# Two-layer cross-attention: the value bias summed under the attention by VectorE, one output product for two batches

## The chip, the cores and the metric

The kernel runs on 1 core of one Trainium2 chip. The metric is the device time of one execution in microseconds (us). The kernel before took 1253.28 us (median of 3 runs, 1253.11 to 1253.95).

## The reference

Two layers follow one another. The change is in the first. Its inputs are `x` and `ctx` (the `y` below), 32 batches of 128 channels by 1024 columns:

```
q, k = Wq y + bq, Wk y + bk;   v = Wv x + bv          # 8 heads of 16 channels
scores = q k^T / sqrt(128)                            # over the 1024 columns: 16x16 per head
attn = softmax(scores)
o = Wo (attn v) + bo + x
h = (o - mean(o)) * rsqrt(var(o) + 1e-5) * gn_w + gn_b   # mean and variance over a whole batch
```

The second layer is an attention with 32 heads over `h` and `ctx`, with low-rank additions to its weights; its output is added to `h`.

## The kernel before, in words

In the first layer the scores don't need q and k themselves. They come from the Gram matrix of a batch, y y^T (128x128), through the weights. The attention of a batch, `att`, is one 128x128 matrix with the heads on its diagonal. Then `n1` = att^T Wo^T and `mix` = Wv^T n1, plus the identity, so that the first layer's output before the norm is mix^T x plus one column, `xbias`:

xbias = Wo (att bv) + bo = n1^T bv + bo

`mix_product` (L614) makes both on TensorE: a product of `wv0` and `n1` (L617), and right behind it a product of `n1` as the weight with the one column `bv_col` (L618), into column 128 of the same bank. `add_mix` (L1241) on VectorE adds the identity (L1244) and adds `bo` to the column (L1245).

The column is used when the batch's mean and variance are made. `partition_stats(b)` on VectorE reads the product mix^T x from two banks (`bn_stats`, L1189, twice; the aggregate, L1191) and adds the column to the mean: `st` (L1193). `stats_product(b)` on TensorE (L589) averages it over the 128 channels with a matrix of 1/128. `deviation(b)` (L1198 to L1201), `norm_factors` (L1211), a power on GpSimd (L1640) and `norm_scale` (L1217, L1220) make the factors with which ScalarE writes `h` (L997).

The order is written out by hand, one program per engine; engines wait for each other by semaphores only. On TensorE one batch b of the first stage is, in order: `gram_products(b)` (L558, 8 matmuls); a preparation of later weights (L547); `turn_gram`, `t1_product` (L600), `turn_k(b-1)`, `score_product(b)` (L605, L607), with chunks 0, 1, 2 of the key and value products `kv_products` (L573, 3 matmuls each) between; `mixed_x(b-1)` (L645, 6 matmuls); chunks 3 and 4; `n1_product(b)` (L612); chunk 5; `mix_product(b)` (L617, L618); `stats_product(b-1)` (L589); chunks 6 and 7. In the last batch (31) transposes of `h` (L663) stand between some of these, and from batch 30 on `var_product` (L594) stands between chunks 6 and 7.

On VectorE one batch is: the Gram matrix put together (L1172, L1177), t1 (L1182), a merge of weights (L1166); `softmax0_begin` (L1228 to L1233), `rest_kT(b-1)` (L1267), `softmax0_end` (L1237, and L1239, which writes `att`); `partition_stats(b-1)`; the first half of the rounding rest of yT for batch b+1 (L1155); `add_mix(b)`; the second half of that rest; `norm_factors(b-2)`, `deviation(b-1)`, `rest_mix(b)` (L1249), `norm_scale(b-2)`.

Small results of TensorE share two banks, 6 and 7. A list built with `use_small` gives the order of use, and each use waits until the one before it in its bank has been read. One tile, `first`, holds the first layer's weights and biases; it is loaded by one DMA at the start, behind the kv factors, the first yT and a quarter of wkv, and ahead of the rest.

Of the kernel before, what the change touches and what calls it, by code (L numbers as in the profile page):

```python
# [8 lines left out]
ALU = mybir.AluOpType  # L9
ACT = mybir.ActivationFunctionType  # L10
AX_X = mybir.AxisListType.X

P = 128
# [4 lines left out]
def xattn_two_layers(nc, x, ctx_4096, ctx_turned, first_layer, wkv_in, w_units, factors_kv, factors_q, factors_o, out):  # L18
# [25 lines left out]
    with ExitStack() as ctx:  # L44
# [52 lines left out]
        def factor_tiles(table, name, dt, *which):  # L97
# [2 lines left out]

        factor_tiles(lora, "lora", F32R, "kv", "o")
        ones_avg = sb("ones_avg", [P, P])
        first = sb("first", [P, 6 * P + 5])
        w0T, wv0, bqk = first[:, 0:3 * P], first[:, 3 * P:4 * P], first[:, 4 * P:6 * P].rearrange("p (a n) -> p a n", a=2)
        score_bias = sb("score_bias", [P, P])
        bq_col, bv_col, bo_col, gnw_col, gnb_col = (first[:, 6 * P + i:6 * P + i + 1] for i in range(5))
        bq_scaled = sb("bq_scaled", [P, 1])
        minus_half = sb("minus_half", [P, 1])
        y_sum = sb("y_sum", [P, 2])
# [1 line left out]
        gram = sb("gram", [P, P])  # L111
        t1 = sb("t1", [P, P])
        s_bq = sb("s_bq", [P, P])
        att = sb("att", [P, P])
        n1 = sb("n1", [P, P])
        mix = sb("mix", [P, P])
# [3 lines left out]
        bn = sb("bn", [P, 2, 6])  # L120
        st, st2, both_st, mv, dev, ve, rstd = (
            norm[:, 0:1], norm[:, 1:2], norm[:, 0:2], norm[:, 2:4], norm[:, 4:5], norm[:, 5:6], norm[:, 6:7])
        xbias, nm, gsc, gbi = ([norm[:, 8 + 2 * k + i:9 + 2 * k + i] for i in range(2)] for k in range(4))
        late_place = at[0]
        factor_tiles(lora, "lora", F32R, "q")
# [86 lines left out]
        def f32(ap):  # L212
# [10 lines left out]
            "wo_out0", "wo_out1", "wo_out2",  # L223
            "yT_hi", "yT_lo", "ysum", "gram_mm", "gram_m", "gram_h", "gram_turn", "gram", "t1_mm", "t1", "sbq",
            "s_mm", "s_sb", "s_max", "s_neg", "s_exp", "s_rec", "att", "n1_mm", "n1", "mix_mm",
            "mix", "mix_hi", "mix_lo", "xbias", "x_hi", "x_lo", "mx_mm", "bn", "agg", "st",
            "st1_mm", "dev", "nm", "st2", "st2_mm", "ve", "pow", "gsc", "gbi", "h", "kv_mm",
            "kv", "kv_keys", "kT_mm", "kT_hi", "kT", "h_out0", "h_out1", "kv_out0", "kv_out1", "stack_ones",
            "h_in0", "h_in1", "hT_mm", "hT_hi", "hT_lo", "q_mm", "q_full", "q_hi", "q_lo", "q_late_hi", "q_late_lo", "k_in0", "k_in1", "k_full", "q_in", "q_late", "q_out0", "q_out1",
# [62 lines left out]
        for b in range(B):  # L292
            if b > 1:
                use_small(7, ("prep", unit_of(b - 1)), ("prep_merged", unit_of(b - 1) + 1))
            for name, done in (("gram", "gram"), ("t1", "t1"), ("s", "s_sb"), ("n1", "n1"), ("mix", "xbias")):
                use_small(6, (name, b), (done, b + 1))
            if b:
                use_small(7, ("st", b - 1), ("nm", b))
            if b - 1 >= LATE_STATS:
                use_small(7, ("var", b - 1), ("ve", b))  # L300
# [228 lines left out]
        def tensor_program(pe):  # L529
# [84 lines left out]
            def mix_product(b):  # L614
                ps = small_bank("mix", b)
                pe.wait_ge(S["n1"], b + 1)
                pe.matmul(ps[:, 0:P], wv0[:], n1[:], start=True, stop=True)  # L617
                pe.matmul(ps[:, P:P + 1], n1[:], bv_col, start=True, stop=True).then_inc(S["mix_mm"], 1)  # L618

            def turn_k(b):  # L620
                ps = small_bank("kT", b)
# [218 lines left out]
            for b in range(1, B):  # L840
                last = b == B - 1
                gram_products(b)
                if b > 1:
                    prep_product(unit_of(b - 1))
                kv_products(b, (0,))
                turn_gram(b)
                kv_products(b, (1,))
                t1_product(b)
                turn_k(b - 1)
                kv_products(b, (2,))  # L850
                score_product(b)
                mixed_x(b - 1)
                kv_products(b, (3,))
                if last:
                    turn_h(0)
                kv_products(b, (4,))
                n1_product(b)
                kv_products(b, (5,))
                if last:
                    turn_h(1)  # L860
                mix_product(b)
                stats_product(b - 1)
                kv_products(b, (6,))
# [39 lines left out]
        def scalar_program(act):  # L903
# [66 lines left out]
            def scale_bias(b):  # L970
                if b:
                    act.wait_ge(S["s_mm"], b)
                else:
                    act.wait_ge(S["first_in"], DMA)
                act.wait_ge(S["ysum"], b + 1)
                act.activation(s_bq[:], bqk[:, 0, :], ACT.Copy, scale=y_sum[:, b % 2:b % 2 + 1]).then_inc(S["sbq"], 1)

            def round_mix(b):
                act.wait_ge(S["mix"], b + 1)
# [157 lines left out]
        def vector_program(dve):  # L1137
# [41 lines left out]
            def evacuate_t1(b):  # L1179
                dve.wait_ge(S["ysum"], b + 1)  # L1180
                dve.wait_ge(S["t1_mm"], b + 1)
                dve.scalar_tensor_tensor(t1[:], bqk[:, 1, :], y_sum[:, b % 2:b % 2 + 1], small["t1", b][:, 0:P],  # L1182
                                         ALU.mult, ALU.add).then_inc(S["t1"], 1)

            def partition_stats(b):
                dve.wait_ge(S["xbias"], b + 1)
                dve.wait_ge(S["mx_mm"], b + 1)
                for half in range(2):
                    dve.bn_stats(bn[:, half, :], mixed_banks(b)[:, half * BANK:(half + 1) * BANK]).then_inc(S["bn"], 1)  # L1189
                dve.wait_ge(S["bn"], 2 * (b + 1))  # L1190
                dve.bn_aggr(mv, bn[:].rearrange("p a b -> p (a b)")).then_inc(S["agg"], 1)  # L1191
                dve.wait_ge(S["agg"], b + 1)
                dve.tensor_scalar(st, mv[:, 0:1], xbias[b % 2], None, ALU.add).then_inc(S["st"], 1)  # L1193

# [46 lines left out]
            def add_mix(b):  # L1241
                ps = small["mix", b]
                dve.wait_ge(S["mix_mm"], b + 1)
                dve.tensor_tensor(mix[:], ps[:, 0:P], ident[:], ALU.add).then_inc(S["mix"], 1)  # L1244
                dve.tensor_tensor(xbias[b % 2], ps[:, P:P + 1], bo_col, ALU.add).then_inc(S["xbias"], 1)  # L1245

            def rest_mix(b):
                dve.wait_ge(S["mix_hi"], b + 1)
# [165 lines left out]
            def prep_lower(n):  # L1414
# [12 lines left out]
            dve.wait_ge(S["first_in"], DMA)  # L1427
            dve.tensor_scalar(bq_scaled[:], bq_col, SCORE0 * L, None, ALU.mult).then_inc(S["bq_scaled"], 1)
            dve.wait_ge(S["bq_scaled"], 1)
            dve.scalar_tensor_tensor(score_bias[:], bqk[:, 1, :], bq_scaled[:], score_bias[:],  # L1430
                                     ALU.mult, ALU.add).then_inc(S["score_bias"], 1)
            begin_gram(0)
            prep_merge(2)
# [8 lines left out]
            softmax0_begin(0)  # L1442
            prep_lower(5)
            softmax0_end(0)
            prep_lower(7)
            rest_yT(1, 0)
            rest_yT(1, 1)
# [2 lines left out]
            for b in range(1, B):  # L1450
# [10 lines left out]
                softmax0_begin(b)  # L1461
                rest_kT(b - 1)
                softmax0_end(b)
                if b == 1:
                    lower_b("q")
                partition_stats(b - 1)
                rest_yT(b + 1, 0)
                if last:
                    split_hT(0)
                add_mix(b)  # L1470
                rest_yT(b + 1, 1)
                if 0 <= b - 2 < LATE_STATS:
                    norm_factors(b - 2)
# [553 lines left out]
def laid_out(inputs):  # L2027
# [4 lines left out]
    y = np.asarray(inputs["ctx_4096"])  # L2032
    size = y.shape[2]
    first = np.concatenate([w0["Wq"].T, w0["Wk"].T, w0["Wo"].T, w0["Wv"],
                            np.broadcast_to(w0["bq"], (P, P)), np.broadcast_to(w0["bk"], (P, P)),
                            np.stack([w0[n] for n in ("bq", "bv", "bo", "gn_w", "gn_b")], axis=1)], axis=1)
    wkv = np.concatenate([w["Wk"], w["Wv"]], axis=1).reshape(size // P, P, -1).transpose(1, 0, 2)

    def heads_last(rows):
# [28 lines left out]
```

## Time and profile before

| | us |
|---|---|
| median of 3 runs | 1253.28 (1253.11 to 1253.95) |
| the profiled execution | 1253.11 |
| its span | 1251.3 |
| TensorE busy | 1239.6 (99%) |
| VectorE busy | 843.2 (67%) |
| ScalarE busy | 807.7 (65%) |
| GpSimd busy | 295.0 (24%) |

The span runs from the first to the last instruction. The first stage takes about the first 343 us of it. In the rows below PE is TensorE's matmuls, PEld its loads of weights, which overlap them; DVE is VectorE, ACT ScalarE, POOL GpSimd. A float32 product on a 128x128 weight shows as two matmul records with two loads. Matmuls are pipelined, so that the lengths of neighbours overlap; the starts of the loads tell how far apart two products are.

### The profile page before, as it was taken

The numbers are of one execution on the slowest core, as the hardware profiler recorded it, in microseconds if no ns is written. First come the engines' busy times: TensorE is split into PE (matmuls) and PEld (weight loads), VectorE is DVE, ScalarE is ACT, GpSimd is POOL, SyncE is SP. The second block draws the span as 40 slices with busy tenths as digits, with TensorE's granted clock in tenths as the row PEclk, the third lists the DMA queues.
The fourth block names the chain that finished last, engine by engine and source line by source line (L and its number), as shares of the span: only waits on it lengthen the run. The fifth ranks groups of instructions, "written<-read, shape, count | busy, mean of one in ns | idle before, by whom it ended". The sixth has DMA issues, their size and how long they took to land.

```text
span 1251.3 us, 24584 instructions
## 1 busy us (share of the span) xinstructions
PE 1239.6 (99%) x7860; PEld 968.7 (77%) x7860; DVE 843.2 (67%) x1953; ACT 807.7 (65%) x2884; POOL 295.0 (24%) x297
## 2 busy tenths in 40 slices
PE   8999999999999999999999999999999999999999
PEld 6788888888887888888878877677776767677677
DVE  6777777777747767767667776776665677766554
ACT  6676776666617887887577877655555577755441
POOL 4444443222233233233333305100000111000000
PEclk9999999999999999999999999999999999999999
DMA  9689899999755445554555559998788999888872
GB/s 329 230 289 290 284 289 336 308 309 311 271 189 167 152 152 175 178 172 152 169 166 181 177 177 333 284 270 239 234 243 236 270 255 257 234 225 244 235 222 85
DMA packets 196590, 291.49 MB, mean 233 GB/s; under 512 B 14160, under 2 KB 119888, under 8 KB 195760
## 3 DMA queue, kind: packets, MB, share of 16 engines
q1 hardware_dynamic: 196464, 289.92, 74.5%
q8 instruction: 65, 1.06, 0.4%
q14 instruction: 61, 0.50, 0.1%
HBM read 183.96 MB, written 105.91 MB: 232 GB/s over the span
## 4 chain that ended last, share of the span: by engine, by line
PE 93%; DVE 4%; issue 1%; DMA 1%; SPq 0%; ACT 0%; DVEq 0%
PE bank L695 28%; PE bank L728 23%; PE bank L573 14%; PE bank L759 5%; PE bank L812 5%; PE bank L795 5%; PE bank L645 3%; PE bank L558 2%; PE bank L663 2%; DMA lora_raw_q<-in_factors_q 1%; PE bank L678 1%; PE bank L600 1%; PE bank L617 1%; PE bank L547 1%; DVE op L1364 1%
## 5 line engine op out<-in xcount | busy, mean ns | idle before, releaser
L1032 ACT ACTIVATE bank<-bank,negs 128x128 f32<-128x128 f32 x1024 | 353.9, 360 | 119.4 <-DVE negs L1314 118.5
L695 PE MATMUL bank<-hT,wq 128*128 128x512 f32 x1488 | 363.8, 396 | 0.0
L728 PE MATMUL bank<-wo,op 128*128 128x512 f32 (+1 forms) x1356 | 346.1, 393 | 2.0 <-DVE h_blk L1408 1.5
L695 PEld LDWEIGHTS bank<-hT,wq 128*128 128x128 f32 x1488 | 273.4, 188 | 60.8
L728 PEld LDWEIGHTS bank<-wo,op 128*128 128x128 f32 x1356 | 252.0, 188 | 62.9 <-issue 6.2
L1053 ACT ACTIVATE probT<-bank 128x512 f32<-128x512 f32 x256 | 152.6, 606 | 169.1 <-PE bank L795 166.5
L1309 DVE TENSOR_REDUCE maxes<-bank 128x4 f32<-128x512 f32 x256 | 175.1, 684 | 94.0 <-PE bank L759 93.6
L1032 ACT ACTIVATION_READ_ACCUMULATOR bank<-bank,negs 128x1 f32 x1024 | 231.3, 226 | 0.0
L573 PE MATMUL bank<-wkv_hi,yT 128*128 128x512 f32 x512 | 198.1, 415 | 0.7 <-POOL wkv_lo L1579 0.5
L1408 DVE TENSOR_TENSOR h_blk<-bank,h_blk 128x512 f32<-128x512 f32 x111 | 76.3, 687 | 95.5 <-PE bank L728 94.6
L573 PEld LDWEIGHTS bank<-wkv_hi,yT 128*128 128x128 f32 x512 | 96.5, 188 | 19.3 <-issue 1.7
L1635 POOL TENSOR_TENSOR k_full<-k_in 128x128 f32<-128x128 f32 x64 | 29.6, 463 | 317.2 <-DMA k_in<-k_dram 269.9
L795 PE MATMUL bank<-q_stack,k_stack 98*128 98x512 f32 x256 | 104.1, 409 | 0.0
L573 PE MATMUL bank<-wkv_lo,yT 128*128 128x512 f32 x256 | 100.3, 392 | 0.0
L1658 POOL TENSOR_TENSOR x_lo<-x_in,x_hi 128x1024 fp32r<-128x1024 f32 x32 | 77.3, 2416 | 18.0 <-ACT x_hi L958 18.0
L795 PEld LDWEIGHTS bank<-q_stack,k_stack 98*128 98x128 f32 x256 | 47.8, 187 | 36.8 <-issue 18.4
L1619 POOL CAST q_part<-q_full 128x512 fp32r<-128x512 f32 x52 | 32.1, 618 | 181.4 <-DVE q_full L1285 181.3
L1366 DVE TENSOR_TENSOR op<-c_sb,op 128x512 fp32r<-128x512 f32 x96 | 67.5, 703 | 3.3
L1621 POOL TENSOR_TENSOR q_part<-q_full,q_part 128x512 fp32r<-128x512 f32 x52 | 66.5, 1280 | 4.2
L1314 DVE TENSOR_SCALAR negs<-maxes 128x4 f32<-128x4 f32 x256 | 47.4, 185 | 27.6 <-DVE maxes L1309 0.5
L1640 POOL TENSOR_TENSOR norm<-norm,minus_half 128x1 f32<-128x1 f32 x32 | 17.6, 551 | 195.3 <-DVE norm L1211 195.3
L1364 DVE TENSOR_SCALAR op<-c_sb 128x512 fp32r<-128x512 f32 x96 | 44.0, 458 | 27.0 <-ACT c_sb L1064 26.0
(148 smaller groups left out, 1659.5 us busy)
## 6 DMA issues: line engine op xcount, KB each, us to landing
q_dram<-q_part SPq DMA_DIRECT2D x96, 512.0 KB, 5.7
q_stack<-q_dram SPq DMA_DIRECT2D x128, 384.0 KB, 4.8
yT_in<-in_ctx_turned SPq DMA_DIRECT2D x32, 512.0 KB, 4.9
y_in<-in_ctx SPq DMA_DIRECT2D x32, 512.0 KB, 7.1
x_in<-in_x SPq DMA_DIRECT2D x32, 512.0 KB, 5.9
h_dram<-h_out SPq DMA_DIRECT2D x32, 512.0 KB, 7.4
h_in<-h_dram SPq DMA_DIRECT2D x32, 512.0 KB, 4.0
h_blk<-h_dram SPq DMA_DIRECT2D x64, 256.0 KB, 5.2
```

Of the source, the lines that this page charges most:

```text
L573: m = pe.matmul(bank(2), yT[b % 2][:, c, part, :], w[:, c, :], start=first, stop=c == final and part == 1)
L695: m = pe.matmul(bank(u % 2).rearrange("p (a n) -> p a n", a=2), wq[:, block, part, c, :], hT[(group + 1) % 2][:, :, of, c, :], start=c == ...
L728: mm = pe.matmul(place[:, columns], op_of(pair, m)[:, of, c, :], wo[m][w][:, c, columns], start=fresh and c == 0 and of == 0 and w == 0, s ...
L759: m = pe.matmul(score_bank(GQ * i + g)[:, j * P:(j + 1) * P], queries, k_full[i % 2][rows, :], start=True, stop=True)
L795: pe.matmul(again_bank(n), k_stack[STACK_ROWS, 2 + k % 2, g, :], again_stack(k)[STACK_ROWS, g, :, :].rearrange("p j n -> p (j n)"), start= ...
L1032: act.activation(part, part, ACT.Exp, bias=negs[:, n % NEGS, j:j + 1], scale=SCORE1, accum_out=sums[:, score_column(k), g, j:j + 1]).then_ ...
L1053: act.activation(probT[prob_place[n]][:], again_bank(n), ACT.Exp, scale=SCORE1).then_inc(S["st_exp"], 1)
L1309: dve.tensor_reduce(largest, score_bank(n).rearrange("p (j t) -> p j t", j=GROUP), AX_X, ALU.max).then_inc(S["max"], 1)
L1366: dve.tensor_tensor(op_part(pair, m, 1), tile, f32(op_part(pair, m, 0)), ALU.subtract).then_inc(S["op_lo"], 1)
L1408: dve.tensor_tensor(h_blk[block][:], made, h_blk[block][:], ALU.add).then_inc(S["o"], 1)
L1621: pool.tensor_tensor(lo, made, f32(hi), ALU.subtract).then_inc(S["q_lo"], 1)
L1658: pool.tensor_tensor(x_lo[:], x_in[b % 2][:], f32(x_hi[:]), ALU.subtract).then_inc(S["x_lo"], 1)
```

## The change

- The tile `first` gets a third broadcast block of biases: `bv` in all 128 rows (`bias_rows[:, 2, :]`), and loses the column `bv_col`. It is 900 columns wide in place of 773.
- `weigh_bias(b)` is new on VectorE: one instruction multiplies `att` by the `bv` rows and sums along the row into one of two columns, `att_bv[:, b % 2]`. In an odd batch it stands right behind `softmax0_end(b)`, ahead of `partition_stats(b-1)`; in an even batch behind `add_mix(b)`; in batch 0 behind `softmax0_end(0)`, ahead of `prep_lower(7)`.
- `bias_product(b)` is new on TensorE, in odd batches only, right behind `n1_product(b)`: the weight Wo^T with the two columns of `att_bv`, for batches b-1 and b.
- `add_bias(b)` is new on VectorE: it adds `bo` to both columns. It stands in `partition_stats(b-1)` of an even b-1, between the aggregate and `st`.
- The product with `bv_col` (L618) and its addition (L1245) are gone. The two columns use bank 7, between the weights' preparation and the statistics.

```diff
-        first = sb("first", [P, 6 * P + 5])
+        first = sb("first", [P, 7 * P + 4])
+        xbias_pair = norm[:, 8:10]
...
-            for name, done in (("gram", "gram"), ("t1", "t1"), ("s", "s_sb"), ("n1", "n1"), ("mix", "xbias")):
+            for name, done in (("gram", "gram"), ("t1", "t1"), ("s", "s_sb"), ("n1", "n1"), ("mix", "mix")):
                 use_small(6, (name, b), (done, b + 1))
+            if b % 2:
+                use_small(7, ("xbias", b), ("xbias", b // 2 + 1))
...
-                pe.matmul(ps[:, 0:P], wv0[:], n1[:], start=True, stop=True)
-                pe.matmul(ps[:, P:P + 1], n1[:], bv_col, start=True, stop=True).then_inc(S["mix_mm"], 1)
+                pe.matmul(ps[:, 0:P], wv0[:], n1[:], start=True, stop=True).then_inc(S["mix_mm"], 1)
+
+            def bias_product(b):
+
+                ps = small_bank("xbias", b)
+                pe.wait_ge(S["att_bv"], b + 1)
+                pe.matmul(ps[:, 0:2], woT0, att_bv[:], start=True, stop=True).then_inc(S["xbias_mm"], 1)
...
                 n1_product(b)
+                if b % 2:
+                    bias_product(b)
                 kv_products(b, (5,))
...
+            def weigh_bias(b):
+
+                dve.wait_ge(S["att"], b + 1)
+                dve.scalar_tensor_tensor(att_bias[:], att[:], 1.0, bias_rows[:, 2, :], ALU.mult, ALU.mult,
+                                         accum_out=att_bv[:, b % 2:b % 2 + 1]).then_inc(S["att_bv"], 1)
+
+            def add_bias(b):
+                dve.wait_ge(S["xbias_mm"], b // 2 + 1)
+                dve.tensor_scalar(xbias_pair, small["xbias", b][:, 0:2], bo_col, None, ALU.add).then_inc(S["xbias"], 1)
+
             def partition_stats(b):
-                dve.wait_ge(S["xbias"], b + 1)
                 dve.wait_ge(S["mx_mm"], b + 1)
...
                 dve.bn_aggr(mv, bn[:].rearrange("p a b -> p (a b)")).then_inc(S["agg"], 1)
+                if b % 2 == 0:
+                    add_bias(b + 1)
+                dve.wait_ge(S["xbias"], b // 2 + 1)
                 dve.wait_ge(S["agg"], b + 1)
...
-                dve.tensor_tensor(xbias[b % 2], ps[:, P:P + 1], bo_col, ALU.add).then_inc(S["xbias"], 1)
...
             softmax0_end(0)
+            weigh_bias(0)
             prep_lower(7)
...
                 softmax0_end(b)
+                if b % 2:
+                    weigh_bias(b)
...
                 add_mix(b)
+                if b % 2 == 0:
+                    weigh_bias(b)
                 rest_yT(b + 1, 1)
```

## Rows read from the trace of the kernel before

**Rows 1.** The page: busy time by engine, and TensorE's granted clock in 40 slices.

```profile
PE 1239.6 (99%) x7860; PEld 968.7 (77%) x7860; DVE 843.2 (67%) x1953; ACT 807.7 (65%) x2884; POOL 295.0 (24%) x297
...
PEclk9999999999999999999999999999999999999999
```

**Rows 2.** Windows: busy us (count) of PE, PEld, DVE, ACT, POOL; clock, DMA.

```profile
180.00:260.00 80.00, 80.00 (x445) 66.72 (x444) 57.16 (x198) 53.48 (x113) 25.84 (x18) 1.00 0.94 316
```

**Rows 3.** Waits of PE from 20 to 350 us: total, times, longest.

```profile
PE bank L558 <- DVE yT L1155: 1.0, 1, 1.0
PE bank L594 <- DVE norm L1201: 0.6, 1, 0.6
...
PE bank L589 <- issue: 0.3, 1, 0.3
```

**Rows 4.** Timeline, TensorE's loads around the statistics: start, length, instruction [idle before].

```profile
184.13 0.30 PEld L589 LDWEIGHTS bank<-norm,ones_avg 128*128 128x128 f32 x2
...
193.82 0.30 PEld L617 LDWEIGHTS bank<-n,first 128*128 128x128 f32 x2 [0.21 <-ACT n L991]
...
194.04 0.30 PEld L618 LDWEIGHTS bank<-first,n 128*128 128x128 f32 x2
...
194.26 0.30 PEld L589 LDWEIGHTS bank<-norm,ones_avg 128*128 128x128 f32 x2
...
194.49 0.19 PEld L573 LDWEIGHTS bank<-wkv_hi,yT 128*128 128x128 f32 x1
```

**Rows 5.** Timeline, VectorE in the same batch, from att on.

```profile
192.04 0.29 DVE L1239 TENSOR_SCALAR att<-att,att_stat 128x128 f32<-128x128 f32 x1
...
192.25 1.29 DVE L1189 BATCH_NORM_STATS2 bn<-bank 128x6 f32<-128x512 f32 x2
...
193.57 0.21 DVE L1191 BATCH_NORM_AGGREGATE norm<-bn 128x2 f32<-128x12 f32 x1
...
193.81 0.22 DVE L1193 TENSOR_SCALAR norm<-norm 128x1 f32<-128x1 f32 x1
...
194.81 0.68 DVE L1155 TENSOR_TENSOR yT<-yT_in,yT 128x512 fp32r<-128x512 f32 x1
```

**Rows 6.** Timeline, the gram loads, and a load that waited for VectorE.

```profile
185.62 1.13 PEld L558 LDWEIGHTS bank<-yT 128*128 128x128 f32 x8
...
188.10 0.29 DVE L1177 TENSOR_TENSOR gram<-bank,gram 128x128 f32<-128x128 f32 x1 [0.37 <-PE bank L581]
...
188.51 0.30 PEld L600 LDWEIGHTS bank<-first,gram 128*128 128x128 f32 x2 [0.25 <-DVE gram L1177]
```

**Rows 7.** Groups by form (busy us, mean ns), then the timeline of an accumulator read.

```profile
L1182 DVE SCALAR_TENSOR_TENSOR t<-first,y_sum,bank 128x128 f32<-128x128 f32 x32 | 11.1, 347 | 22.4 <-PE bank L600 22.4
...
L1430 DVE SCALAR_TENSOR_TENSOR score_bias<-first,bq_scaled,score_bias 128x128 f32<-128x128 f32 x1 | 0.4, 351 | 0.0
...
191.63 0.19 ACT L984 ACTIVATION_READ_ACCUMULATOR att<-att,att_stat 128x1 f32 x1
191.72 1.05 ACT L967 ACTIVATE lora_kv<-y_in 128x1024 fp32r<-128x1024 f32 x1
```

**Rows 8.** DMA issues (KB each, us to landing); timeline of the start.

```profile
first<-in_first_layer SPq DMA_DIRECT2D x1, 386.5 KB, 6.8
...
17.44 1.05 ACT L910 CAST lora_q<-lora_raw_q 96x1024 fp32r<-96x1024 f32 x1 [0.94 <-DMA lora_raw_q<-in_factors_q]
...
19.32 0.68 DVE L1417 TENSOR_TENSOR wkv_lo<-wkv_raw,wkv_hi 128x512 fp32r<-128x512 f32 x1
...
30.65 0.68 DVE L1155 TENSOR_TENSOR yT<-yT_in,yT 128x512 fp32r<-128x512 f32 x1
30.80 2.78 POOL L1658 TENSOR_TENSOR x_lo<-x_in,x_hi 128x1024 fp32r<-128x1024 f32 x1 [5.47 <-ACT x_hi L958]
...
31.51 2.61 DVE L1155 TENSOR_TENSOR yT<-yT_in,yT 128x512 fp32r<-128x512 f32 x1
```

**Rows 9.** Timeline, the first transposes of h in batch 31.

```profile
335.26 0.60 PE L663 MATMUL bank<-ident,h_in 128*128 128x128 f32 x4
```

More of the change, by code:

```diff
@@ L102, in xattn_two_layers @@
         ones_avg = sb("ones_avg", [P, P])
-        first = sb("first", [P, 6 * P + 5])
-        w0T, wv0, bqk = first[:, 0:3 * P], first[:, 3 * P:4 * P], first[:, 4 * P:6 * P].rearrange("p (a n) -> p a n", a=2)
+        first = sb("first", [P, 7 * P + 4])
+        w0T, wv0, bias_rows = first[:, 0:3 * P], first[:, 3 * P:4 * P], first[:, 4 * P:7 * P].rearrange("p (a n) -> p a n", a=3)
         score_bias = sb("score_bias", [P, P])
-        bq_col, bv_col, bo_col, gnw_col, gnb_col = (first[:, 6 * P + i:6 * P + i + 1] for i in range(5))
+        bq_col, bo_col, gnw_col, gnb_col = (first[:, 7 * P + i:7 * P + i + 1] for i in range(4))
         bq_scaled = sb("bq_scaled", [P, 1])
@@ L113, in xattn_two_layers @@
         s_bq = sb("s_bq", [P, P])
+        att_bias = sb("att_bias", [P, P])
+        att_bv = sb("att_bv", [P, 2])
         att = sb("att", [P, P])
@@ L225, in xattn_two_layers @@
             "s_mm", "s_sb", "s_max", "s_neg", "s_exp", "s_rec", "att", "n1_mm", "n1", "mix_mm",
-            "mix", "mix_hi", "mix_lo", "xbias", "x_hi", "x_lo", "mx_mm", "bn", "agg", "st",
+            "mix", "mix_hi", "mix_lo", "att_bv", "xbias_mm", "xbias", "x_hi", "x_lo", "mx_mm", "bn", "agg", "st",
             "st1_mm", "dev", "nm", "st2", "st2_mm", "ve", "pow", "gsc", "gbi", "h", "kv_mm",
@@ L975, in scale_bias @@
                 act.wait_ge(S["ysum"], b + 1)
-                act.activation(s_bq[:], bqk[:, 0, :], ACT.Copy, scale=y_sum[:, b % 2:b % 2 + 1]).then_inc(S["sbq"], 1)
+                act.activation(s_bq[:], bias_rows[:, 0, :], ACT.Copy, scale=y_sum[:, b % 2:b % 2 + 1]).then_inc(S["sbq"], 1)
             def round_mix(b):
@@ L1181, in evacuate_t1 @@
                 dve.wait_ge(S["t1_mm"], b + 1)
-                dve.scalar_tensor_tensor(t1[:], bqk[:, 1, :], y_sum[:, b % 2:b % 2 + 1], small["t1", b][:, 0:P],
+                dve.scalar_tensor_tensor(t1[:], bias_rows[:, 1, :], y_sum[:, b % 2:b % 2 + 1], small["t1", b][:, 0:P],
                                          ALU.mult, ALU.add).then_inc(S["t1"], 1)
+            def weigh_bias(b):
[5 more added lines that the diff above has]
+                dve.tensor_scalar(xbias_pair, small["xbias", b][:, 0:2], bo_col, None, ALU.add).then_inc(S["xbias"], 1)
             def partition_stats(b):
-                dve.wait_ge(S["xbias"], b + 1)
                 dve.wait_ge(S["mx_mm"], b + 1)
@@ L1429, in vector_program @@
             dve.wait_ge(S["bq_scaled"], 1)
-            dve.scalar_tensor_tensor(score_bias[:], bqk[:, 1, :], bq_scaled[:], score_bias[:],
+            dve.scalar_tensor_tensor(score_bias[:], bias_rows[:, 1, :], bq_scaled[:], score_bias[:],
                                      ALU.mult, ALU.add).then_inc(S["score_bias"], 1)
@@ L2034, in laid_out @@
     first = np.concatenate([w0["Wq"].T, w0["Wk"].T, w0["Wo"].T, w0["Wv"],
-                            np.broadcast_to(w0["bq"], (P, P)), np.broadcast_to(w0["bk"], (P, P)),
-                            np.stack([w0[n] for n in ("bq", "bv", "bo", "gn_w", "gn_b")], axis=1)], axis=1)
+                            np.broadcast_to(w0["bq"], (P, P)), np.broadcast_to(w0["bk"], (P, P)), np.broadcast_to(w0["bv"], (P, P)),
+                            np.stack([w0[n] for n in ("bq", "bo", "gn_w", "gn_b")], axis=1)], axis=1)
     wkv = np.concatenate([w["Wk"], w["Wv"]], axis=1).reshape(size // P, P, -1).transpose(1, 0, 2)
```

## The prediction

> **What bounds the kernel now.** I read the page first, then the first stage by windows, then who waits for whom on TensorE, then one batch in order of time, because the change touches only the first stage. TensorE (PE) is busy 99% of the span and its clock is granted in full [rows 1]. In the middle of the first stage it is busy 80.00 of 80 us while VectorE (DVE) has 57.2 [rows 2]. In all of that stage PE is named as waiting in five places, once each and for 0.3 to 1.0 us (the first two and the last are shown); for the product of the statistics that was once [rows 3]. So the stage is bound by the order and number of PE's instructions; one batch takes 194.26 - 184.13 = 10.13 us [rows 4]. Two things follow: each PE instruction saved is worth its full slot, and each new wait of PE costs its full length. PE being busy does not say how close the next wait is, so the batch has to be read closely.
>
> Three loads of weights stand at 193.82 (mix), 194.04 (bias column), 194.26 (statistics) and the next at 194.49 [rows 4]. Each float32 product on a 128x128 weight is two passes and takes a slot of 0.22 us, even that with one column: it is the weight load, not the columns, that sets it.
>
> The statistics product needs DVE's `st`, whose last instruction starts at 193.81 and takes 0.22, so it ends at 194.03 [rows 5]. From a DVE result to PE's load takes 0.12 us: gram ends at 188.10 + 0.29 = 188.39, the load that waited for it starts at 188.51 [rows 6]. So the load of the statistics could start at 194.15 and starts at 194.26: the slack is 0.11 us. That is the number that decides here. The chain behind `st` is DVE alone, in order: att scaled at 192.04, two bn_stats at 192.25, the aggregate at 193.57, `st` at 193.81 [rows 5].
>
> **The change part by part.** The profiled execution took 1253.11 us, 1.8 more than its span of 1251.3, and 0.17 under the median of the three times; my sum is a difference to it.
>
> (a) Removed on PE: 32 bias-column products of one slot. 32 x 0.22 = -7.0 us. Added: 16 products for two batches, 16 x 0.22 = +3.5 us. By slots alone the change gives -3.5 us.
>
> (b) Even batches (2 to 28, 14 of them). The column's slot stood just before the statistics. Without it their load would start at 194.04 on the scale of the rows, but `st` lets it go only at 194.15. So only 0.22 - 0.11 = 0.11 us is gained: 14 x -0.11 = -1.5 us. The rest of the slot turns into a wait. The new weighing comes here after mix on DVE, not ahead of `st`. It pushes the second half of yT, which starts at 194.81 and ends at 195.49 [rows 5], by 0.2 to 0.45 us. The gram products of the next batch start at 185.62 + 10.13 = 195.75 and need that half after four of eight loads, at about 196.3 [rows 6]: ready at 196.0 at worst, it stays hidden. If the cover went, it would cost the difference.
>
> (c) Odd batches (3 to 29, 14 of them). DVE now does two things between att and `st`.
> The weighing (128x128, both inputs in SBUF, with a sum) waits for att's end, 0.29 + 0.03 after att's start. An independent instruction follows a 128x128 one after 0.21 (192.04 to 192.25), so bn_stats starts 0.32 + 0.21 after att's start in place of 0.21: +0.32 us, if the sum is free. DVE shows no sum of this form. Nearest rows: the same operation without a sum takes 0.35 with a scalar pointer [rows 7]; ScalarE's read of its accumulator takes 0.19 [rows 7], of which, with the next instruction at 191.72, 0.09 delay it. So the bounds are 0.32 and 0.55 (0.32 + 0.19 and a little), and I take 0.42, the row of ScalarE's delay added. It can't be below nothing, as the instruction stands in order before bn_stats.
> The bias add (128x2 with a pointer) stands between the aggregate and `st`, which waits for it. Such an instruction takes 0.22 [rows 5]. If it overlapped the aggregate so far as to start 0.08 behind its start, it would end at 193.87 and `st` start at 193.90: +0.09, the low end by an assumed overlap. If it starts only after the aggregate, +0.22. I take 0.15.
> Together `st` comes 0.57 later (0.41 to 0.77), and the load of the statistics goes at 194.15 + 0.57 = 194.72 in place of 194.26. PE's own work is equal here: one slot (the new product, right behind n1) for one slot (the column). So each odd batch loses 0.46 us (0.30 to 0.66): 14 x 0.46 = +6.4 us. The new product's own wait is smaller: the sum is ready by 192.36 + 0.29 + 0.19 + 0.12 = 192.96, and its load is due behind n1's, about 193.1. Queued behind the waiting statistics on PE are the last two chunks of keys and values and the next batch's gram; nothing there lets PE catch up, since it had no idle time to give back. DVE's later instructions (yT, mix, deviation) move by 0.5 with PE moving by 0.46, so no second wait forms; the start of the next batch has DVE idle and takes in its lag. The statistics product also waits for the bias add through the shared bank, but that ends before `st`.
>
> (d) The two last batches. In batch 30 the variance product waits 0.6 us for DVE already [rows 3]; the even-batch weighing stands ahead of it, +0.3 us (0.2 to 0.4). Batch 31 has two groups of four transposes of h between the attention and the statistics, each 0.60 long with what overlaps it, together well over the 0.46 of an odd batch [rows 9]: 0.
>
> (e) The start. The `first` tile grows by 127 columns, 65 KB on 386.5 [rows 8], ahead of the q factors on the same queue; ScalarE waits 0.94 us for these at 17.44 [rows 8] and only then does the exponents of batch 0: 0 to 0.2 us. The weighing of batch 0 stands on DVE ahead of the rounding rest at 19.32, for which PE's last chunk waits: +0.35, less the column's 0.22. In batch 1 (odd) both DVE additions again stand ahead of `st` and of the two yT halves, where PE waits 1.0 us [rows 3]. The second half took 2.61 us there in place of 0.68, since GpSimd's subtraction of x (30.80, 2.78 us) ran [rows 8]; the first half, started at 30.65 ahead of GpSimd, took 0.68 [rows 8]. Pushed by 0.5 us more than GpSimd, the first half falls behind it too, and the end of the second moves from 34.12 to some 35.2. Start in all: +0.9 us (0.3 to 1.4; low if the first half still escapes).
> The Trainium skill ("SBUF — State Buffer", section "Who interferes with whom") says that a VectorE instruction with two SBUF inputs is blocked whole by a GpSimd instruction that reads SBUF. The trace agrees in size (2.61 beside 0.68); by it batch 1 costs 1.1, without it 0.5.
>
> Sum: -1.5 + 6.4 + 0.3 + 0.9 = +6.1 us. 1253.11 + 6.1 = 1259.2 us. Its own range, with all terms at their ends: -1.8 + 4.2 + 0.2 + 0.3 = +2.9 to -1.2 + 9.2 + 0.4 + 1.4 = +9.8, so 1256.0 to 1262.9. The other stages keep their work and their order.
>
> **Rivals.**
> 1. The slots come through: -3.5 us, 1249.8. For it: PE is saturated and DVE only 71% busy in the stage [rows 2]; DVE's shorter chain could absorb the additions if bn_stats overlapped the weighing. Against: the slack of 0.11 us [rows 4 to 6] is shorter than any DVE instruction. It decides from `st` at most 0.1 us later.
> 2. Give and take: the additions on DVE are at or under their low ends, the even batches keep most of the slot, and the start is cheap: with 0.25 lost in odd and 0.18 gained in even batches 14 x 0.07 + 0.5 = +1.5, so about 1254.6 (1252.5 to 1255.9). For it: all my bounds hang on overlaps of 0.1 us. Against: it needs three of them at once.
> 3. Dearer sum: the weighing runs at half speed. Rows show a column at (0.68 - 0.29)/384 = 1.0 ns (yT's 512 columns against att's 128 [rows 5]); twice that is +0.13 us in each odd batch, +1.9 in all, 1261.1. It also puts the new product's wait at its edge. Against: the same operation without a sum shows nothing of it, 0.351 with two SBUF inputs and 0.347 with one [rows 7]. The Trainium skill ("Vector Engine (DVE) Microarchitecture Reference", section "Points that are easy to get wrong") says that this operation with two sources in SBUF wider than bf16 runs at half throughput, as no port is left for the accumulator; no row before has the sum, so it stays open.
> 4. The change does not save the slot: the column's weights were hidden behind other matmuls. Rows speak against it, 0.22 us between loads; it would only add the waits, some 1263, and I fold it into the high end.
>
> **How the numbers follow.** Forecast 0.53, rival 3 with 4 0.14, rival 2 0.20, rival 1 0.13. The likeliest gives 1259.2. A difference under 0.2% (2.5 us, about what a measurement of this kernel can tell from none) is the same: 1250.8 to 1255.8. The forecast's own range begins at 1256.0, so slower has 0.67, same 0.20, faster 0.13. The range for 8 in 10 leaves out rival 1 (0.13) and the upper tail (0.06): 1252.2 to 1262.5.
>
> **What would show it.** Right: PE waits for DVE's `st` ahead of the statistics in nearly all batches, about 0.45 us in odd and 0.1 in even ones; the period of two batches goes from 20.26 to about 20.6 us; `st` starts about 0.55 later behind att in odd batches; 32 fewer passes of PE in the stage (64 gone, 32 new). The second stage keeps its length. Wrong: a period of two batches of 20.04 and no wait at the statistics is rival 1; a wait at the new product in place of the statistics means that the sum is much dearer than 0.55; a changed second stage would mean that something other than these steps moved the time.

## The result and the profile after

The changed kernel took 1263.26 us (median of 4 runs, 1261.43 to 1265.49) against 1253.19 us before (4 runs): a ratio of 1.0075, 95% interval 1.0063 to 1.0087. It is slower by 10.1 us. I had forecast slower, 1259.2 us, with a range to 1262.5. The direction and the place were right, the size was not.

The page of the profile after (its execution took 1265.49 us, the slowest of the four), as in [rows 1]:

```profile
span 1263.7 us, 24584 instructions
...
PE 1245.6 (99%) x7828; PEld 969.2 (77%) x7828; DVE 851.0 (67%) x2001; ACT 808.2 (64%) x2884; POOL 294.8 (23%) x297
...
PEclk9999999999999999999999999999999999999999
```

TensorE has 32 matmul records fewer (7860 to 7828), as the change meant, and its busy time grew all the same, by 6 us. A busy share of 99% before and after says nothing about the loss. The question of [rows 3], who kept TensorE waiting, asked from 20 to 360 us, says more (total, times, longest):

```profile
PE bank L594 <- DVE norm L1217: 2.4, 5, 1.1
PE bank L594 <- issue: 1.8, 10, 0.2
```

L594 is the statistics product (L589 before), L1217 is `st`. Fifteen waits where there was one. Still 4.2 us are not 10: this list counts only the idle time between modelled matmuls, and it has no row for what a slower clock costs. The starts of the weight loads give the full account. From one statistics load to the next, in us:

| | before | after |
|---|---|---|
| batch 1 (start) to batch 2 | 30.80 to 42.23 | 32.74 to 44.65 |
| an even batch, median | 10.13 | 10.19 |
| an odd batch, median | 10.13 | 10.545 |
| 14 even batches (4 to 30) | 141.89 | 142.97 |
| 14 odd batches (3 to 29) | 141.88 | 148.18 |
| batch 31 | 12.09 | 12.25 |
| the last statistics load | 346.77 | 356.75 |

So of 9.98 us at the end of the first stage 2.42 come from the start, 1.08 from even batches, 6.30 from odd ones and 0.2 from the end. The rest of this execution took 906.95 us after that load in place of 904.5. In the changed kernel's variants below it took 904 to 906, and I put nothing down to it. This execution was 2.2 us above the median of its four, so the 9.98 us of the first stage fit the 10.1 us between the medians.

An even batch after, in order of time (the answer of [rows 4 and 5]):

```profile
189.47 0.21 DVE L1212 BATCH_NORM_AGGREGATE norm<-bn 128x2 f32<-128x12 f32 x1
...
189.76 0.30 PEld L622 LDWEIGHTS bank<-n,first 128*128 128x128 f32 x2 [0.21 <-ACT n L1003]
189.79 0.21 DVE L1217 TENSOR_SCALAR norm<-norm 128x1 f32<-128x1 f32 x1
...
190.23 0.30 PEld L594 LDWEIGHTS bank<-norm,ones_avg 128*128 128x128 f32 x2 [0.17 <-issue]
```

Two numbers differ from what I had read before. `st` starts 0.32 behind the aggregate (189.47 to 189.79); before it was 0.24. And it ends at 190.00 while the load starts at 190.23: 0.23 us, not the 0.12 of [rows 6]. It is so in each of the 28 batches from 3 to 30 (0.220 to 0.227). The idle time is put down to "issue", so the profile names nothing that the engine waited for there.

An odd batch after:

```profile
198.11 0.29 DVE L1263 TENSOR_SCALAR att<-att,att_stat 128x128 f32<-128x128 f32 x1
...
198.44 0.29 DVE L1200 SCALAR_TENSOR_TENSOR att_bias<-att,first 128x128 f32<-128x128 f32 x1
...
198.65 0.08 DVE L1200 DVE_READ_ACCUMULATOR att_bias<-att,first 128x1 f32 x1
198.65 1.29 DVE L1210 BATCH_NORM_STATS2 bn<-bank 128x6 f32<-128x512 f32 x2
...
199.18 0.30 PEld L628 LDWEIGHTS bank<-att_bv,first 128*128 128x128 f32 x2
...
199.98 0.21 DVE L1212 BATCH_NORM_AGGREGATE norm<-bn 128x2 f32<-128x12 f32 x1
200.10 0.17 DVE L1205 TENSOR_SCALAR norm<-bank,first 128x2 f32<-128x2 f32 x1
...
200.30 0.21 DVE L1217 TENSOR_SCALAR norm<-norm 128x1 f32<-128x1 f32 x1
...
200.74 0.30 PEld L594 LDWEIGHTS bank<-norm,ones_avg 128*128 128x128 f32 x2 [0.35 <-issue]
```

bn_stats starts 0.54 behind att in place of 0.21 [rows 5]: the weighing costs 0.33. Its sum costs nothing: bn_stats starts in the same instant as the read of the accumulator, 0.21 behind the weighing (198.44 to 198.65). The bias add starts 0.12 behind the aggregate's start, and `st` stands 0.32 behind the aggregate as in even batches. Together `st` comes 0.41 later, and the batch is 0.41 longer. The new product (L628) does not wait.

### The profile page after: what moved, and what is told of

The parts are those of the page before. It is cut to its first block, busy times and chain, and to the rows that moved or that the text cites. A ratio compares the mean times of both kernels' runs of the same rounds, so it can differ in the third digit from the quotient of the medians.

```text
span 1263.7 us, 24584 instructions
## 1 busy us (share of the span) xinstructions
PE 1245.6 (99%) x7828; PEld 969.2 (77%) x7828; DVE 851.0 (67%) x2001; ACT 808.2 (64%) x2884; POOL 294.8 (23%) x297
## 4 chain that ended last, share of the span: by engine, by line
PE 90%; DVE 5%; issue 2%; DMA 2%; SPq 1%; ACT 0%; DVEq 0%
PE bank L705 27%; PE bank L738 21%; PE bank L578 13%; PE bank L769 5%; PE bank L822 5%; PE bank L805 4%; PE bank L655 3%; PE bank L563 2%; PE bank L673 2%; DMA lora_raw_q<-in_factors_q 1%; PE bank L688 1%; DVE op L1387 1%; PE bank L594 1%; PE bank L605 1%; DVE c_sb L1406 1%
## 5 line engine op out<-in xcount | busy, mean ns | idle before, releaser
L822 PE MATMUL bank<-probT,v_in 128*32 128x512 f32 x512 | 62.0, 599 | 0.0
```

The source lines that it names most:

```text
L822: m = pe.matmul(context_bank(k)[g * HD:(g + 1) * HD, :], v_in[:, k % 2, g, :], probT[prob_place[GQ * k + g]][:], start=True, stop=True)
```

## The experiments

Twelve kernels ran. "Before" is the median of the kernel before on the same chip, measured together with the run. The column "even / odd" is the median distance between statistics loads, "first stage" the time of the last of them (346.77 before, 356.75 after).

| run | us | before | ratio (95%) | even / odd | first stage |
|---|---|---|---|---|---|
| a_st2_first | 1260.01 | 1253.64 | 1.0053 (1.0038 to 1.0068) | 10.085 / 10.43 | 353.78 |
| a_stats_late | 1252.56 | 1253.64 | 0.9992 (0.9982 to 1.0001) | 9.95 / 10.12 | 347.20 |
| b_no_column | 1253.48 | 1253.64 | 0.9999 (0.9990 to 1.0009) | 10.11 / 10.11 | 346.68 |
| a_double | 1266.10 | 1253.64 | 1.0100 (1.0084 to 1.0117) | 10.185 / 10.89 | 360.45 |
| b_wide_first | 1254.39 | 1254.52 | 1.0000 (0.9991 to 1.0009) | 10.145 / 10.16 | 347.59 |
| a_waits_early | 1262.48 | 1254.52 | 1.0065 (1.0051 to 1.0079) | 10.12 / 10.55 | 355.95 |
| a_late_weigh0 | 1253.37 | 1254.52 | 0.9994 (0.9985 to 1.0004) | 9.95 / 10.12 | 345.21 |
| a_best | 1257.54 | 1254.52 | 1.0026 (1.0016 to 1.0036) | 9.95 / 10.12 | 350.12 |
| a_four_moves | 1252.29 | 1254.32 | 0.9985 (0.9976 to 0.9994) | 9.94 / 10.11 | 344.57 |
| a_weigh0_late | 1262.64 | 1254.32 | 1.0066 (1.0051 to 1.0081) | 10.19 / 10.535 | 354.91 |
| b_no_column_late | 1248.43 | 1254.32 | 0.9955 (0.9940 to 0.9970) | 9.935 / 9.93 | 341.89 |
| b_stats_late | 1254.60 | 1254.32 | 1.0004 (0.9995 to 1.0013) | 10.15 / 10.15 | 347.31 |

**Is the loss the wait at the statistics?** Moved out of its reach:

```diff
                 mix_product(b)
-                stats_product(b - 1)
+                if b - 1 >= LATE_STATS:
+                    stats_product(b - 1)
                 kv_products(b, (6,))
+                if b - 1 < LATE_STATS:
+                    stats_product(b - 1)
```

> The changed kernel with the statistics product of batches 0 to 28 moved on TensorE from behind the mix product to behind key and value chunk 6, 0.7 us later. Theory G (the whole loss of the loop is the statistics product waiting for VectorE): both kinds of batch lose their wait, even 9.91 and odd 10.13 us, a pair 20.04 in place of 20.73, so 14 x 0.69 = -9.7 us, about 1253.6; the start stays 2.4 us late. Rival (the loss sits elsewhere, in the order of matmuls or in VectorE's later work): the periods stay near 10.19 and 10.53, time 1260 to 1264.

Measured: 9.95 and 10.12, 1252.56 us. One product 0.7 us later takes back the loss of the loop and, of the 3.1 us that its slots are worth, 2.4 besides (28 batches in 281.3 us, before 283.8). Theory G holds. The control, the same edit on the kernel before:

> The kernel before with the statistics product behind chunk 6 and nothing else, as a control of that move. Theory G (before, TensorE did not wait there, so the move alone gives nothing): period 10.13, the time of the kernel before. Rival (the move is itself a gain, and the late version of the changed kernel owes its time to it): below 10.08, 1.5 us or more faster.

Measured: 10.15, ratio 1.0004. The move by itself gives nothing.

**Is it VectorE's chain that is late?** The weighing done twice in odd batches:

```diff
                                          accum_out=att_bv[:, b % 2:b % 2 + 1]).then_inc(S["att_bv"], 1)
+                if b % 2:
+                    dve.wait_ge(S["att_bv"], b + 1)
+                    dve.scalar_tensor_tensor(t1[:], att[:], 1.0, bias_rows[:, 2, :], ALU.mult, ALU.mult,
+                                             accum_out=att_stat[:, 3:4])
```

> The changed kernel with the weighing done twice in odd batches (the second one waits for the first, writes to tiles that nobody reads then). Theory G (VectorE's chain up to st is what odd batches wait for): each odd batch grows by the length of one more weighing, 0.33 us, 10.53 to 10.86, 14 x 0.33 = +4.6 and some at the start, about 1268.2. Rival (the weighing is covered, the loss of the odd batches comes from the order of the waits or from the new product): 1263.3 to 1264.

```profile
200.10 0.29 DVE L1200 SCALAR_TENSOR_TENSOR att_bias<-att,first 128x128 f32<-128x128 f32 x1
...
200.31 0.08 DVE L1200 DVE_READ_ACCUMULATOR att_bias<-att,first 128x1 f32 x1
...
200.65 1.29 DVE L1214 BATCH_NORM_STATS2 bn<-bank 128x6 f32<-128x512 f32 x2
```

The rows are of this kernel's odd batch. bn_stats now starts 0.34 behind the first accumulator read. The odd batch grew by 0.345 (10.545 to 10.89), the even one not at all. What was added to this chain was added to the batch. The time, 1266.10 us, stayed under the 1268.2 expected. The first stage ends 3.7 us later than in the changed kernel: two batches that were long by 0.4 us there (9 and 24) are regular here, and the start was 0.5 shorter in this execution.

**How much slack was there before the change?** This is the step that failed. The column product taken out of the kernel before, with VectorE's instructions kept:

```diff
-                pe.matmul(ps[:, 0:P], wv0[:], n1[:], start=True, stop=True)
-                pe.matmul(ps[:, P:P + 1], n1[:], bv_col, start=True, stop=True).then_inc(S["mix_mm"], 1)
+                pe.matmul(ps[:, 0:P], wv0[:], n1[:], start=True, stop=True).then_inc(S["mix_mm"], 1)
...
-                dve.tensor_tensor(xbias[b % 2], ps[:, P:P + 1], bo_col, ALU.add).then_inc(S["xbias"], 1)
+                dve.tensor_tensor(xbias[b % 2], ps[:, 0:1], bo_col, ALU.add).then_inc(S["xbias"], 1)
```

> The kernel before without the column product on TensorE (one slot of 0.22 us per batch); the addition of bo reads column 0 of mix instead, so the value bias is left out of the result. VectorE's instructions are the same in number and form. Theory Z (no slack at all in front of the statistics, since st reaches the load 0.23 us after its end): the period stays at 10.13 us, time 1253.2. Rival of my prediction (slack 0.11): 10.02 us, 31 x -0.11 = -3.4, 1249.8. Rival that slots come through: 9.91 us, -6.8, 1246.4.

`st` and the loads of mix and statistics in this kernel:

```profile
193.79 0.21 DVE L1192 TENSOR_SCALAR norm<-norm 128x1 f32<-128x1 f32 x1
193.81 0.30 PEld L617 LDWEIGHTS bank<-n,first 128*128 128x128 f32 x2 [0.21 <-ACT n L990]
...
194.23 0.30 PEld L589 LDWEIGHTS bank<-norm,ones_avg 128*128 128x128 f32 x2
```

Thirty-two products fewer and the same time. The loads of mix and statistics are 0.42 apart where 0.22 would do, and the second starts 0.23 behind the end of `st`, in this batch and in the 27 others (0.221 to 0.227). In the kernel before it stood 0.226 to 0.268 behind. There was no slack before, or 0.04 us at the most: the column product filled a gap that was there anyway. With the same edit and the statistics moved:

> The kernel before without the column product (the value bias is left out of the result) and with the statistics product behind chunk 6 in batches 0 to 28. Theory G with slots of 0.22: with the wait out of the way the slot comes through, period 9.91 us in all batches of the loop, 30 x -0.22 = -6.6 us, about 1247. Rival (a slot with one column is partly covered by its neighbours): 10.0 or more, 1250 or more.

Measured: 9.93 in all batches, 1248.43 us, ratio 0.9955 (-5.9 us). So a slot is worth 0.2 us, but only once the statistics are out of the way.

**Why 0.23 and not 0.12?** In `stats_product` a wait for `st2`, long satisfied, stands behind the wait for `st`; in `t1_product`, from which I had the 0.12, the late wait is the last. Swapped in the changed kernel:

```diff
+                pe.wait_ge(S["st2"], b)
                 pe.wait_ge(S["st"], b + 1)
-                pe.wait_ge(S["st2"], b)
```

> The changed kernel with the order of two waits swapped in the statistics product on TensorE: the wait for st2 (long satisfied) now stands ahead of the wait for st, not behind it. Nothing else differs. Theory A (a satisfied wait that stands behind the late one costs TensorE about 0.11 us, which is why st reaches the load after 0.23 us and not the 0.12 of my prediction): even batches go from 10.19 to about 10.08 us, odd ones from 10.53 to 10.42, 30 x 0.11 = -3.3 us, so about 1260.0. Rival (0.23 us is the latency of this product whatever the order): periods and time stay, 1263.3.

An even batch of this kernel, `st` and the load that needs it:

```profile
188.28 0.21 DVE L1217 TENSOR_SCALAR norm<-norm 128x1 f32<-128x1 f32 x1
...
188.61 0.30 PEld L594 LDWEIGHTS bank<-norm,ones_avg 128*128 128x128 f32 x2
```

0.12 us (0.115 or 0.116 in 27 of the 28 batches), periods 10.085 and 10.43, 1260.01 us. Two lines changed places and 3 us came back. The intervals of the two ratios just overlap (1.0053 and 1.0075, four executions each); the periods carry the finding. Theory A holds.

**Why is `st` 0.08 late in even batches?** The change put the wait for xbias between the aggregate and `st`. Moved back ahead of bn_stats in even batches:

```diff
             def partition_stats(b):
+                if b % 2:
+                    dve.wait_ge(S["xbias"], b // 2 + 1)
...
                     add_bias(b + 1)
-                dve.wait_ge(S["xbias"], b // 2 + 1)
+                    dve.wait_ge(S["xbias"], b // 2 + 1)
```

> The changed kernel with VectorE's wait for xbias moved ahead of the two bn_stats in even batches, where it has long been satisfied (the kernel before has it there); in odd batches it stays, as the addition of bo is really late. Theory W (that wait, standing behind the aggregate, is what puts st 0.08 us later in even batches): st starts 0.24 behind the aggregate in even batches in place of 0.32, their period goes from 10.19 to 10.11, odd ones keep 10.54; 14 x -0.08 = -1.1 us, about 1262. Rival (the 0.06 us over 10.13 of even batches is something else): 10.19 stays, 1263.3.

The aggregate and `st` in an even batch of this kernel:

```profile
189.29 0.21 DVE L1214 BATCH_NORM_AGGREGATE norm<-bn 128x2 f32<-128x12 f32 x1
...
189.53 0.21 DVE L1219 TENSOR_SCALAR norm<-norm 128x1 f32<-128x1 f32 x1
```

0.24 again, and the even batch went from 10.19 to 10.12. It is not quite the same thing as on TensorE: here the satisfied wait (xbias) stood ahead of the late one (the aggregate), and it cost time all the same, because it stood between two instructions of which the second waits for the first. In the time it is too small to be told (ratio 1.0065 against 1.0075); the rows show it.

**The start.** It lost 2.4 us where I had 0.9. The rows of the changed kernel:

```profile
32.08 2.37 POOL L1686 TENSOR_TENSOR x_lo<-x_in,x_hi 128x1024 fp32r<-128x1024 f32 x1 [5.89 <-ACT x_hi L970]
32.30 0.21 DVE L1217 TENSOR_SCALAR norm<-norm 128x1 f32<-128x1 f32 x1 [0.43 <-DVE norm L1205]
32.43 2.56 DVE L1167 TENSOR_TENSOR yT<-yT_in,yT 128x512 fp32r<-128x512 f32 x1
...
32.77 0.35 PE L594 MATMUL bank<-norm,ones_avg 128*128 128x2 f32 x2 [1.11 <-DVE norm L1217]
...
35.12 0.68 DVE L1167 TENSOR_TENSOR yT<-yT_in,yT 128x512 fp32r<-128x512 f32 x1
```

As foreseen, the first half of yT fell behind GpSimd, which before it had escaped [rows 8]. But TensorE did not wait for it: the wait of 1.0 us for yT [rows 3] is gone, as TensorE itself came later. What I had not foreseen is in the windows (us; busy of PE, PEld, DVE, ACT, POOL; clock, DMA, GB/s), of the changed kernel:

```profile
32.00:36.00 4.00, 3.17 (x12) 2.31 (x13) 3.70 (x7) 0.77 (x4) 2.37 (x1) 0.74 0.95 342
36.00:40.00 4.00, 4.00 (x21) 3.32 (x21) 1.49 (x6) 1.97 (x6) 0.00 (x0) 0.83 0.84 301
```

and of the one that has only the weighing of batch 0 moved (a_weigh0_late):

```profile
32.00:36.00 4.00, 3.33 (x19) 2.99 (x20) 3.07 (x9) 1.36 (x5) 1.31 (x1) 1.00 1.03 338
36.00:40.00 4.00, 4.00 (x23) 3.23 (x22) 2.44 (x8) 2.59 (x5) 0.00 (x0) 1.00 0.95 330
```

The granted clock averages 0.74 and 0.83 in these windows: between the level of 2.4 GHz and that of 1.2 GHz. What is missing to 1.00 adds up to 1.7 us of TensorE's time (4 x 0.26 + 4 x 0.17), so it was at the lower level for 3.4 us. It fell after TensorE had waited 0.60 and 1.11 us in batch 1. Three runs on the start. In the first the only edit is the one of this diff, in the second it stands beside the later statistics product:

```diff
-            weigh_bias(0)
             prep_lower(7)
...
             add_mix(0)
+            weigh_bias(0)
```

> The changed kernel with only the weighing of batch 0 moved behind mix of batch 0. Theory S (the start's 2.4 us come from that one instruction: it delays the last key and value chunk, by this the x of batch 1, and puts the first half of yT behind GpSimd's subtraction): the statistics load of batch 1 goes from 44.65 to 42.8 or so, the loop keeps 10.19 and 10.54, time 2 us less than the changed kernel, about 1261.3. Rival (the start also needs the statistics moved): 44 or more, 1263.

> The changed kernel with the statistics product behind chunk 6 (as in the run before that had it alone: 1252.56, first stage 0.4 us longer than before) and, new, the weighing of batch 0 moved on VectorE from ahead of the rounding rest for which TensorE's last chunk waits to behind mix of batch 0. Theory S (that weighing costs its 0.33 us at the start): TensorE's first batch loses 0.3 us of wait, 1252.2. Rival (the loads arrive late anyway and hide it): 1252.6.

The third is the kernel before with a wider tile:

```diff
-        first = sb("first", [P, 6 * P + 5])
+        first = sb("first", [P, 7 * P + 4])
```

> The kernel before with the tile of first-layer weights widened by 127 columns of zeros that nobody reads, to the size that it has in the changed kernel (450 KB in place of 386.5); no instruction differs. Theory D (part of the start's 2.4 us is this load, which stands ahead of wkv, y and the q factors in the same queue, since in the changed kernel the q factors landed 0.65 us later): the statistics load of batch 1 goes from 42.23 to 43.0 or later, time 1254.3 to 1255. Rival (the start is lost to the weighings of batches 0 and 1 alone): 42.2 to 42.4, time 1253.5.

The second statistics load came at 42.82 in a_weigh0_late (44.65 in the changed kernel) and at 42.92 in a_late_weigh0 (44.93 in a_stats_late). In the profiles of all five kernels with the weighing of batch 0 ahead of the rounding rest, the clock fell between 32 and 40 us; in the eight others without a_best it did not. The same five, and none of the eight, have this wait of TensorE for the rounding rest that stands behind the weighing (here the changed kernel's; 0.48 us in each):

```profile
21.14 0.47 PE L578 MATMUL bank<-wkv_hi,yT 128*128 128x512 f32 x1 [0.48 <-DVE wkv_lo L1440]
```

So the profiles agree on some 1.9 us. In the first pair they are the clock's: the first statistics loads are 0.11 us apart (32.74 and 32.63), although y for batch 2 landed 1.6 us later in the changed kernel (ScalarE waited for it 1.65 us there and 0.16 in a_weigh0_late). The other 1.72 us arise between the first and the second load, where TensorE has no wait of 0.15 us or more in either kernel, and they are what the two windows lost. The chain that I gave in the expectation (that weighing delays x of batch 1 and so on) is not what the rows show: in a_weigh0_late the first half of yT was blocked too (1.53 us), and the clock stayed.

The times don't confirm the 1.9 us: a_weigh0_late took 1262.64 us, nearer the rival's 1263 than the 1261.3 of theory S, and a_late_weigh0 1253.37. The ratios 1.0066 against 1.0075 and 0.9994 against 0.9992 allow it in the first pair and hardly in the second. Nor did the clock fall in every execution: of the 26 of these five kernels 12 had a mean clock of 1.000, and 3.4 us at the lower level would make it 0.999. In a_st2_first three such executions took 1259.03, 1260.39 and 1260.88 us and the profiled one, with the fall, 1259.62. What the fall is worth in the time is not shown. The wider tile gave no difference in the time (ratio 1.0000), and in its profile the second statistics load was 0.45 us later (42.68), between theory D and its rival; theory D is not borne out.

**The best version.** The statistics behind chunk 6, both waits reordered and weighing 0 moved were put together, first also with the bv rows in a DMA of their own behind the loads of the start (this part of the edit is shown):

```diff
             load_raw(FIRST_Q + 1)
+            sp.dma_start(bv_rows[:], bv_in).then_inc(S["bv_in"], DMA)
...
             def weigh_bias(b):
+                if b == 0:
+                    dve.wait_ge(S["bv_in"], DMA)
```

> Everything that the runs point to at once: the changed kernel with the statistics product behind chunk 6, st2's wait ahead of st's, VectorE's xbias wait ahead of bn_stats in even batches, the weighing of batch 0 behind mix, and the bv rows in a tile and a DMA of their own, sent behind all loads of the start, so that first is 384.0+2 KB wide as before. Theories G, D and S together: the loop keeps -0.18 us in even batches (14 x 0.18 = -2.5), the start loses only batch 1's weighing (0.3 to 0.8), so about 1251.3 (1250.5 to 1252). If the start's loss is none of these: 1252.5. If batch 1's chain brings back all: 1253.

The weighing of batch 0 and the t1 product of batch 1 in that kernel's timeline, then its window:

```profile
23.35 2.44 DVE L1206 SCALAR_TENSOR_TENSOR att_bias<-att,bv_rows 128x128 f32<-128x128 f32 x1 [1.25 <-DMA bv_rows<-in_bv]
...
27.84 0.46 PE L606 MATMUL bank<-first,gram 128*128 128x128 f32 x2 [3.35 <-DVE gram L1193]
```

```profile
28.00:32.40 4.40, 4.40 (x17) 3.78 (x17) 1.69 (x7) 1.92 (x5) 0.00 (x0) 0.61 1.00 284
```

That DMA was an error of mine: the bv rows landed 15.4 us after their issue, the weighing waited 1.25 us for them in front of all of VectorE's work, started behind GpSimd's subtraction and took 2.44 us in place of 0.29. TensorE waited 3.35 us, and in the window after it the clock was at 0.61 on average. The whole loop's gain was gone. Without that DMA:

> The best of the last two calls without the separate load of the bv rows, on which VectorE had waited 1.25 us and then been blocked by GpSimd: the changed kernel with the statistics product behind chunk 6, st2's wait ahead of st's, VectorE's xbias wait ahead of bn_stats in even batches, the weighing of batch 0 behind mix. Theories G and S: a loop of 281.1 us (283.8 before), no loss at the start, so 1.7 to 2.5 us less than the kernel before of the same call. Rival (the start's loss comes back through batch 1): the same as before.

One odd batch of its timeline, `st` and the load of the statistics:

```profile
192.68 0.21 DVE L1222 TENSOR_SCALAR norm<-norm 128x1 f32<-128x1 f32 x1
...
193.27 0.42 PEld L594 LDWEIGHTS bank<-norm,ones_avg 128*128 128x128 f32 x2
```

The load of the statistics now starts 0.38 behind the end of `st`, in its turn. Measured: 1252.29 us against 1254.32, ratio 0.9985 (0.9976 to 0.9994): 2.0 us less than before the change, and the only version with all of the computation whose interval lies wholly below the kernel before. The kernel before with the same reordered waits was not run, so what the new computation alone contributes to the 2.0 us is not shown.

## Why the prediction was wrong

- Right: what bounds the kernel, and where the change would be paid. The loop's loss is the statistics product waiting for `st` (a_stats_late, a_double), the second stage kept its length within the scatter (904 to 907 us after the last statistics load, in all fourteen profiles), and the new product doesn't wait.
- (b), even batches, failed. The prediction said: "So the load of the statistics could start at 194.15 and starts at 194.26: the slack is 0.11 us." The latency of 0.12 was read from a product whose late wait is its last. The statistics product has a satisfied wait behind the late one, and needs 0.23: there was next to no slack, as b_no_column shows. So the 0.11 gained per even batch was not there. On top the change's own order of waits put `st` 0.08 later (a_waits_early), and batch 24 was 0.4 us longer than its kind. Forecast -1.5 us over 14 batches, measured +1.1. This step has 2.6 of the 4.1 us between forecast and result.
- (c), odd batches: the mechanism was right, and the total by luck, from errors that cancel. `st` was 0.41 late, the low end of my 0.41 to 0.77, as the sum came free and the bias add cost no more than the wait for it, 0.08. With no slack all of it reached the batch: 14 x 0.41 = 5.7 us. Batches 3 and 9, longer than their kind by 0.2 and 0.4 us, make up the rest. Forecast +6.4, measured +6.3.
- (e), the start: forecast +0.9, in the profile +2.4. Of this 1.94 us stand at the first statistics load: 0.42 was there at 16 us already (TensorE's first wait for GpSimd, 15.97 before and 16.39 after), 0.48 is the new wait at 21 us, 0.77 the longer wait at the statistics (0.34 before, 1.11 after), and small differences are the rest. The other 0.48 lie between the first and the second load: 1.7 lost by the clock, 1.0 given back because TensorE no longer waited for yT, 0.2 by the slot. So the wait for yT, on which most of the term was built, is not where it was lost, and the clock was not in the term. That the clock fell for some 3.4 us in this execution and in the profiles of the four other kernels with the early weighing is shown; why it did so there and not in a_weigh0_late, where TensorE's longest wait was 1.95 us and so longer, is open.
- (d), the last two batches: 0.2 of the forecast 0.3.
- Rival 3, the weighing at half speed, is out: 0.288 us (32 of them) with two sources in SBUF and a sum, less than the 0.347 and 0.351 of [rows 7]. Here the measurement contradicts what the Trainium skill ("Vector Engine (DVE) Microarchitecture Reference", section "Points that are easy to get wrong") says of this operation: half throughput with two sources in SBUF that are not bf16.
- The upper end of the range was 0.8 us too low, because it stood on a slack of 0.11 in all 28 batches; without it (28 x 0.11 = 3.1) the same sum gives 1262.3 with an upper end of 1265.6. That would still have been near for a poor reason, with the odd batches 1.7 us too dear and the start 1.5 too cheap.

What stays open: two batches of the changed kernel (9 and 24) were 0.4 us longer than their kind, and the same two in most variants, but neither in a_double nor in a_best. In batch 9 VectorE's read of the scores starts 0.36 us later than in batch 7, and in batch 24 ScalarE's copy of the Gram matrix 0.26 later than in batch 22, behind TensorE products that stand where they do in those batches. What held them is not shown.

## What to carry to other kernels

Before an instruction of the bounding engine is called a gain, find what the next one on that engine waits for; if its operand comes no earlier, the slot turns into a wait (32 products taken out here: nothing). Of several waits ahead of one instruction the late one should be the last, and a wait long satisfied should stand ahead of earlier work, not between two instructions of which the second waits for the first; here that was 0.11 us on TensorE and 0.08 on VectorE, each time. A latency read from one place holds only for a place with the same waits behind it. A product whose result is not urgent is better placed a little later than its operand can be ready.

## What the hardware showed that I had not expected

- A satisfied wait behind a late one cost TensorE 0.11 us (0.23 to 0.12 in a_st2_first). On VectorE one that stood ahead of the late one, between the aggregate and `st`, cost 0.08 us (0.32 to 0.24 in a_waits_early).
- VectorE's sum along a row was all but free here: the read of the accumulator takes 0.08 us, and an independent instruction starts in the same instant (198.65).
- The granted clock fell for some 3.4 us after waits at the start (0.74 and 0.83 in two windows of 4 us), in an execution whose mean is 0.999 and whose 40 slices all show 9; it showed in narrow windows only. In a_best it was 0.61 over 4.4 us behind a wait of 3.35 us.
